# A 16-image attention and expert kernel whose score operands are copied head by head inside the on-chip memory, with the last scores paired across the array's two halves

## The reference, cut to what matters

```
q, k, v, t = split(layernorm(x) @ W_qkv, 4)          # to heads: (8, 1024, 16)
dots  = einsum('hid,hjd->hij', q, k) * 16 ** -0.5
out1  = einsum('hij,hjd->hid', softmax(dots), v)
```

## Time and profile before

| | |
|---|---|
| median of 3 runs | 2686.31 us (2678.34 to 2692.49) |
| the profiled execution: its time / its span | 2669.74 us / 2667.9 us |
| TensorE busy | 2220.1 us (83%) |
| VectorE / ScalarE / GpSimd busy | 1835.4 / 1492.9 / 1021.2 us |
| mean granted clock of TensorE | 0.877 of full |
| moved by DMA | 265.37 MB |

### The profile page before, as it was taken

The page is one execution under the profiler, slowest core; times in us unless marked ns, Lnnn a source line. Parts: engine busy times, 40 slices in busy tenths (PEclk is TensorE's granted clock), DMA queues, the critical chain, the costliest instruction groups (busy, mean ns, idle before and its releaser), DMA issues.

```text
span 2667.9 us, 35340 instructions
## 1 busy us (share of the span) xinstructions
PE 2220.1 (83%) x12448; PEld 990.7 (37%) x12448; DVE 1835.4 (69%) x2613; ACT 1492.9 (56%) x2897; POOL 1021.2 (38%) x1479
## 2 busy tenths in 40 slices
PE   2789999999999999999989999999897277777744
PEld 1333333333334343333433333333333165555533
DVE  5667887877878787887878778788721455555532
ACT  1146877767677676767767676667653033333320
POOL 2202215434242434424244342431313455565654
PEclk9998999989989898998989899899965588887875
DMA  5422244131323313133231313320102366555549
GB/s 195 108 37 63 55 92 137 31 98 39 98 87 59 104 29 100 38 95 94 55 104 33 96 41 100 89 57 14 49 19 73 113 221 205 170 163 166 167 138 346
DMA packets 97913, 265.37 MB, mean 99 GB/s; under 512 B 21008, under 2 KB 41176, under 8 KB 91160
## 3 DMA queue, kind: packets, MB, share of 16 engines
q1 hardware_dynamic: 75312, 218.04, 29.9%
q0 software_dynamic: 17280, 35.95, 3.9%
q10 hardware_dynamic: 5144, 9.13, 0.9%
HBM read 154.63 MB, written 111.56 MB: 100 GB/s over the span
## 4 chain that ended last, share of the span: by engine, by line
PE 63%; ACT 10%; issue 8%; another core or an unknown queue 6%; POOL 4%; DMA 3%; DVE 3%; SPq 2%; ACTq 1%; POOLq 0%; DVEq 0%
PE ps L880 27%; PE ps L894 19%; ACT region L1170 5%; PE ps L837 3%; PE ps L845 1%; POOL y_dram L767 1%; PE ps L849 1%; PE ps L859 1%; PE ps L914 1%; DMA region<-y_dram 1%; PE ps L903 1%; PE ps L927 1%; PE ps L1023 1%; DVE row_max L1417 1%
## 5 line engine op out<-in xcount | busy, mean ns | idle before, releaser
L1417 DVE TENSOR_REDUCE row_max<-ps 128x1 f32<-128x1024 f32 x1024 | 1235.4, 1216 | 342.3 <-PE ps L859 227.3
L1170 ACT ACTIVATE region<-ps 128x512 f32<-128x512 f32 x2048 | 1115.6, 596 | 567.7 <-PE ps L880 499.2
L880 PE MATMUL ps<-big 50*128 50x512 f32 x2048 | 896.2, 499 | 97.1 <-ACT region L1170 67.1
L859 PE MATMUL ps<-big 48*128 48x512 f32 x2048 | 883.6, 499 | 25.8 <-DMA big<-k_rows 20.3
L880 PEld LDWEIGHTS ps<-big 50*128 50x128 f32 x2048 | 364.2, 200 | 816.9 <-ACT region L1170 631.8
L894 PE MATMUL ps<-region 128*32 128x512 f32 (+1 forms) x4992 | 635.9, 585 | 0.3 <-ACT region L1170 0.3
L859 PEld LDWEIGHTS ps<-big 48*128 48x128 f32 x2048 | 361.0, 201 | 49.5 <-DVE row_max L1417 25.1
L767 POOL DMA_INDIRECT y_dram<-region x284 | 272.5, 960 | 201.5 <-ACT region L1251 123.6
L712 POOL DMA_INDIRECT xs_dram<-region,slot x256 | 249.7, 975 | 80.8 <-issue 71.7
L1023 PE MATMUL ps<-big 128*128 128x512 f32 x284 | 139.6, 492 | 110.8 <-DMA big<-w_dram 37.8
L697 POOL TENSOR_TENSOR region<-region 128x256 f32<-128x256 f32 x64 | 44.8, 734 | 441.1 <-DVE region L1463 441.1
(11 more groups left out here) (182 smaller groups left out, 2026.4 us busy)
## 6 DMA issues: line engine op xcount, KB each, us to landing
big<-w_dram SPq DMA_DIRECT2D x71, 514.0 KB
big<-q_rows SPq DMA_DIRECT2D x64, 384.0 KB, 8.7
big<-k_rows SPq DMA_DIRECT2D x64, 384.0 KB, 9.8
region<-xs_dram SPq DMA_DIRECT2D x71, 264.0 KB
q_rows<-q_parts SPq DMA_DIRECT2D x16, 1024.0 KB, 4.2
k_rows<-k_parts SPq DMA_DIRECT2D x16, 1024.0 KB, 6.5
region<-y_dram SPq DMA_DIRECT2D x16, 1024.0 KB, 9.9
region<-in_x SPq DMA_DIRECT2D x28, 512.0 KB, 6.2
```

Source lines behind the costliest of these rows:

```text
L859: mm = pe.matmul(ps[:, M_BANK + 2 * (n % 2) + c, :], lane_rows(q_stack[k % 2], h, SHIFT_ROW)[:, t * P:(t + 1) * P], lane_rows(k_stack[k % ...
L880: pe.matmul(ps[:, E_BANK + i, :], lane_rows(k_stack[k % 2], h, STACK)[:, t * P:(t + 1) * P], lane_rows(q_stack[k % 2], h, STACK)[:, c * BA ...
L1170: act.activation(probs[:, u % 2, 2 * p + i, :], ps[:, E_BANK + i, :], ACT.Exp, scale=DH ** -0.5).then_inc(exp_done, 1)
L1417: dve.tensor_reduce(row_max[:, h * TILES + t:h * TILES + t + 1], ps[:, at:at + 2, :], AX.XY, ALU.max).then_inc(max_done, 1)
```

## The change

The two DRAM tensors and `rows_to_dram` go. `load_stacks` copies from the tiles of parts straight into the stacks: for each of q and k, each of four heads and each of the three stacked parts one DMA of 16 rows of 1024 elements (64 KB), so 24 DMAs per group in place of four, and 48 per image in place of twelve. The columns of the q and k weights keep their order by head (before they were ordered by channel within the head). For group 0 of image 0 SP issues the twelve of q and ScalarE, before its loop, the twelve of k. `projected` now waits until both groups of the stacks of the image before have landed. In the last image, from step 26 (`ALONE`), step_head gives a step one head of each half of the rows: heads 0 and 2 at an even step, 1 and 3 at an odd one; the exponentials go to the places of these heads.

```
+Q_ORDER, K_ORDER = (0, 0, 1), (0, 1, 0)
+ALONE = 26
-        q_rows = dram("q_rows", (PAIRS, P, TOK))
-        k_rows = dram("k_rows", (PAIRS, P, TOK))
-        STACK_INC = 2 * LANES * 16
+        STACK_INC = 2 * PAIRS * GROUP * 16
+        def stack_rows(n, k, g):
+            stk, parts, order = ((q_stack, q_parts, Q_ORDER), (k_stack, k_parts, K_ORDER))[n]
+            for h in (0, 2, 1, 3):
+                h += g * GROUP
+                for pair, part_no in enumerate(order):
+                    row = lane_of(h) * LANE + pair * DH
+                    yield (stk[k % 2][row:row + DH, h // GROUP * LANE_HEADS + h % LANE_HEADS, :].bitcast(F32),
+                           parts[h * DH:(h + 1) * DH, part_no, :].bitcast(F32))
+        def step_head(k, s, i):
+            if k == IMAGES - 1 and s >= ALONE:
+                return LANE_HEADS * i + s % 2
+            return LANE_HEADS * (s % 2) + i
-            def rows_to_dram(k):
...
-            def load_stacks(k, g):
-                sp.wait_ge(rows_out, (k + 1) * ROWS_INC)
+            def load_stacks(k, g, kinds=2):
                 if k >= 2:
                     sp.wait_ge(score_ready, 2 * (k - 2) * STEPS + (g + 1) * STEPS)
-                for lane in range(LANES):
...
+                for n in range(kinds):
+                    sp.wait_ge(qk_split, 2 * k + n + 1)
+                    for to, rows in stack_rows(n, k, g):
+                        sp.dma_start(to, rows).then_inc(stack_in[k % 2][g], 16)
-            rows_to_dram(0)
-            load_stacks(0, 0)
+            load_stacks(0, 0, 1)
             for it in range(-1, IMAGES + 1):
                 if it + 1 < IMAGES:
-                    if it < 0:
-                        sp.wait_ge(stack_in[0][0], STACK_INC)
                     load_stacks(it + 1, 1)
...
-                if it + 2 < IMAGES:
-                    rows_to_dram(it + 2)
             def scores(k, s, i):
-                g, c, t, p = s // 32, s // 16 % 2, s // 2 % TILES, s % 2
-                h = g * GROUP + LANE_HEADS * p + i
+                g, c, t = s // 32, s // 16 % 2, s // 2 % TILES
+                h = g * GROUP + step_head(k, s, i)
                     act.wait_ge(qk_split, 2 * k)
-                    act.wait_ge(rows_out, k * ROWS_INC)
+                    for g in range(GROUPS):
+                        act.wait_ge(stack_in[(k - 1) % 2][g], ((k - 1) // 2 + 1) * STACK_INC)
-                    act.activation(probs[:, u % 2, 2 * p + i, :], ps[:, E_BANK + i, :], ACT.Exp,
+                    act.activation(probs[:, u % 2, step_head(k, s, i), :], ps[:, E_BANK + i, :], ACT.Exp,
                                    scale=DH ** -0.5).then_inc(exp_done, 1)
                 projected("k", 0, c, k_f, k_parts)
+            act.wait_ge(qk_split, 2)
+            for to, rows in stack_rows(1, 0, 0):
+                act.dma_start(to, rows).then_inc(stack_in[0][0], 16)
-        "wq": by_dim(qkvt[:, 0:P]), "wk": by_dim(qkvt[:, P:2 * P]), "wv": c(qkvt[:, 2 * P:3 * P]),
+        "wq": c(qkvt[:, 0:P]), "wk": c(qkvt[:, P:2 * P]), "wv": c(qkvt[:, 2 * P:3 * P]),
```

More of the change, by code:

```diff
@@ L399, in build @@
         q_high = sem("q_high")
-        rows_out = sem("rows_out")
         stack_in = [[sem(f"stack_in{n}{g}") for g in range(GROUPS)] for n in range(2)]
@@ L466, in build @@
         CONST_INC = 16 * len(consts)
-        ROWS_INC = 2 * PARTS * 16
-        STACK_INC = 2 * LANES * 16
+        STACK_INC = 2 * PAIRS * GROUP * 16
         SHIFT_INC = PARTS * LANES * 16
@@ L1683, in laid_out @@
         w2_blocks[g * HID:(g + 1) * HID, g * CP_SPLIT:(g + 1) * CP_SPLIT] = w["L0_conv_W2"][g].T
-    def by_dim(m):
-        return c(m.reshape(P, HEADS, DH).transpose(0, 2, 1).reshape(P, P))
     return {
```

## The result

The changed kernel takes 2651.28 us (median of 4 runs, 2642.64 to 2664.79) against 2682.32 us for the kernel before (4 runs, 2676.89 to 2692.49) in the same comparison: a ratio of 0.9890, interval 0.9848 to 0.9931, so 31 us less, between 18 and 41. (Ratios leave out the few executions that took over 1.5% longer than the fastest of their kernel: two of the ten of the kernel with pairs from step 40, and one of the 25 of the kernel before beside it.) Forecast were 2672.1 us, 14.2 less, in a range of 2654 to 2686.

The account below looks back on a forecast made before the run. TensorE bounds the loop (0.92 clock) and the last image (0.50); a DRAM chain bounds the start. Gains 6.5 + 0 + 7.7 = 14.2 us from the 2686.3 median give 2672.1, range 2654 to 2686.

Parts of the forecast that it names:

- Part 1, the start: Start of kernel: without k's DRAM round trip, first score at 73.6 (69.5 to 74.6); gain 6.5 us.
- Rival C: Start: small 16-row copies are slow, first score at 80.8, nothing won there; total gain 7 to 9, 2678; chance 0.20.
- The estimate from the port rule: Start: 16 partitions reach four ports, 0.60 us per 64 KB copy; 24 copies end at 78.7, gain 1.4 us.
- Part 2, the loop: Image loop: removed DRAM traffic stood on no chain, added issues (10.6 us per group) are covered; zero, -3 to +3 us.
- Rival E: Start and loop: copy rate goes by rows, ScalarE waits before q_parts in each round; slower, 2740 us; chance 0.08.
- Part 3, the pairs at half clock: Last image: two scores in different halves free TensorE 0.43 us earlier where work lies between; 7.7 us, bounds 0 to 16.
- rival B: Last image: denser pairs let TensorE return to 2.4 GHz; 8 us on top, 2664 us; chance 0.17.
- The test written for the forecast: Forecast wrong if the start moves under 4 us, or step 26 to the end shrinks under 5 or over 11.
- the forecast's own bound: Last image: full clock through all of the stage would give 27 us on top.

Follow-up runs that it names:

- Stacks alone: Changed kernel with ALONE = 64: stacks copied straight from the tiles, no pairs in the last image; 2678.53 us, 0.9986 of the kernel before.
- the filler: Changed kernel without pairs, plus one unread matmul beside each score from step 28 of the last image: 2632.82 us, 0.9907; with pairs 2630.04 us, 0.9907.
- the shared start: Changed kernel with the twelve first k copies split, six on SP ahead of group 1's q copies and six on ScalarE; 2638.84 us, measured once.

## Why the prediction was wrong, step by step

**Part 1, the start: right in kind, short by a quarter.** Forecast 6.5 us (73.6 for the first score), measured 4.7 (75.34), which is above the upper bound of 74.6. The mis-sized term is the spacing of the issues. It was taken from four loads of 48 rows, 0.44 us; the new copies stand 0.64 apart, so that twelve take 7.65 us and not 5.3. They also began at 63.12 and not at 62.4. What follows the last issue was overestimated: 75.21 - 70.77 = 4.4 us to the landing, where 73.6 - 67.7 = 5.9 had been allowed, so that the total was only 1.7 late. The gain carries: VectorE's shift of image 0 comes at 135.6 on average in the three profiles with stacks through DRAM (137.3, 135.1, 134.3) and at 130.5 in the eight with the new ones and ScalarE's twelve issues (128.5 to 132.7; 131.5 in the three of them on the first chip).

Rival C, which had the first score at 80.8, did not come. The estimate from the port rule of the Trainium skill ("SBUF — State Buffer", Door 1) was 78.7. It let all 24 copies move one after another, 14.4 us and a landing. By the trace the twelve of k had landed at 75.21, 12.1 us after 63.12, and their issues alone took 7.65 of that. With the issues shared the first score came at 70.76. So the sum over 24 copies does not hold here; the estimate of 0.60 us for a single copy is not tested by these runs, since the issues stand further apart than that.

**Part 2, the loop: not contradicted.** Stacks alone give 0.9986 (0.9952 to 1.0020), start included, and the loops of the profiles differ by up to 27 us for one and the same program, so the forecast's zero, with 3 us either way, could not be tested as a number. The waits are as forecast. The issues took 15.2 us in place of 10.6 per group, the same mis-sized term, and this too was covered: ScalarE's copy of q_parts at 1001.03 shows no wait for a DMA. The load of the input started at 1044.22, forecast 1044.3, but by two errors that cancel, an earlier begin (1028.44 against 1032.89) and slower issues. Rival E had asked for copies of more than 1.05 us each; the copies' median landing is 2.4 us and they overlap.

**Part 3, the pairs at half clock: right in size.** The pair, the projection (3.45) and the turnings (4.55) are as forecast to a hundredth; the plain steps stay, as forecast. Only the cut values gain less, 1981.78 - 1979.76 = 2.02 per step where 1.85 was guessed. In all: the last stretch of the profile after is 100.8 - 87.9 = 12.9 us shorter. Of these the spell of full clock from 2010.48 to 2020.32 gives about 5.6: what runs in its 9.84 us takes at half clock 0.92 for a pair, 2 x 4.55, 1.87 for values and 3.51 for the logits (2024.10 - 2020.59 in the trace before), 15.4. That leaves 7.3 us for the pairs in this one profile; forecast 7.7.

**The step that failed: the sum held the clock at 0.50 through the last image.** Its term for the clock was nothing; the return stood outside, as rival B, with a chance of 0.17 and a price of 8 us. It returned in each of the ten profiles with pairs or filler and in none of the three without. Over the five profiles of kernels with all pairs and no filler the last stretch is 79.4 us on average ((87.9 + 76.8 + 77.6 + 77.0 + 77.5) / 5) against 100.5, so 21.2 less (80.6 and so 20.0 less for the three on the first chip). With 7.3 for the pairs, which is their worth at half clock, the clock gives about 14 us. Two arguments against B failed. "The values and the side work, which fill most of the stage, stay the same" is true and did not decide, since what stands between them became denser, and TensorE reached 2.4 GHz for spells. And I gave B less because TensorE was busy 98% of the time without having the clock, as though more work could then do nothing; the filler brought it back, at a busy share no higher (71.91 of 76.10 us).

The Trainium skill ("TensorE: Matmul & The Clock Gate", Part 1) says that activity releases the throttle. By that rule the traces with the filler agree in direction, 72 matmuls more and 0.78 in place of 0.52; those of before do not, if activity is read as busy time (rows 1). I had used that mismatch to mark the rival down rather than to ask what had to change for the clock to rise.

The sum by the profiles: 5.1 for the start (135.6 - 130.5), 21.2 for the last stretch and 1.9 for the stretch from there to the first matmul of the experts (79.3 on average in the three without pairs, 77.4 in the five with; not explained) are 28.2 us. The loop is left out of this sum, because its length scatters by as much. The measured gain is 31, in 18 to 41; the two repeats on one chip each gave 22 (first chip) and 29 (third chip) between medians. The test written for the forecast (start moved by at least 4 us, last stretch shorter by 5 to 11) failed on its second half, by this mechanism.

**Left open.** What of the work the clock follows, and whether both halves must be at work. Why it falls back after the logits (step 53) in all profiles but the two with filler and pairs on the third chip, where it stays at 1.00 to the last values. And the 1.9 us behind the last values.

## What to carry to other kernels

Where a stretch is bound by TensorE at half clock, the price of half clock can be the largest term (here 100 us that full clock would shorten by up to 27, by the forecast's own bound), and a change that makes the matmuls denser should be priced with the clock at both levels, whatever the busy share says. Doing the same scores two at a time in the two halves of the rows gained 7 us by itself and 14 more through the clock. A filler can win the same clock, but what it wins has to be measured in the whole kernel; here it was not told from the changed kernel. Copies in many small DMAs should be priced by the issue spacing of their own form. Sharing them between two queues brought the first score 3.7 us forward, and no gain of the whole was shown for it.

## What the runs showed of the hardware that was not expected

- TensorE at 0.52 of its clock with a busy share of 96% over the last stretch of the kernel with stacks alone (96.97 of 100.80 us), brought to 0.78 by matmuls whose results are not read, one beside each score, in the rows that the score leaves free. The stretch got 24.7 us shorter by the work added.
- SBUF to SBUF copies of 16 rows (64 KB) are issued 0.63 to 0.64 us apart on SP and ScalarE alike (in the shared start 0.7 on ScalarE and 0.8 on SP); loads of 48 rows from DRAM 0.44 to 0.47. The copies' median time from issue to landing is 2.4 us.
- The three chips differ by 9% in the same program (2680.79, 2651.75, 2451.35 us for the kernel before), and the granted clock is a part of it only. Windows of the changed kernel in the loop and in the experts on the first chip:

```profile
300.00:900.00 600.00, 558.62 (x3491) 210.84 (x3487) 482.93 (x661) 428.70 (x799) 221.97 (x371) 0.94 0.23 49
2150.00:2500.00 350.00, 247.31 (x1087) 187.37 (x1088) 189.81 (x270) 122.52 (x323) 209.03 (x218) 0.86 0.58 181
```

and on the third:

```profile
300.00:900.00 600.00, 581.25 (x3737) 224.94 (x3735) 520.54 (x708) 455.74 (x853) 232.61 (x390) 0.97 0.25 54
...
1950.00:2300.00 350.00, 263.03 (x1278) 210.87 (x1279) 229.08 (x328) 139.96 (x377) 241.16 (x254) 0.91 0.71 222
```

The third chip does 7% more matmuls in the same 600 us of the loop, at a clock 3% higher, and 18% more in 350 us of the experts, at a clock 6% higher. The rest is idle time. Between the shifts of the first and the last image the first chip's trace of the changed kernel (its second profile) has 24 gaps of over 1.5 us between TensorE's records, 57 us in all, of which the longest are over 4 us; the third chip's has 3, 7.7 us in all. What causes them the traces do not show. The ratio of the two kernels is alike on all three, 0.9869 to 0.9911.
